# Normalising stage: units of four consecutive tokens, one bank and one copy for each half, loops written out

## What is computed

```python
h = h + _L0_attn_ref(_layernorm(h, axis=-1), gamma, W_in, b_in, conv_w, A, Bp, C, W_out, b_out)
h = h + _L0_ffn_ref(_layernorm(h, axis=-1), Ws, bs, W1, b1, W2, b2)

def _L0_attn_ref(x, gamma, W_in, b_in, ...):
    rms = jnp.linalg.norm(x, axis=-1, keepdims=True) * x.shape[-1] ** (-0.5)
    xn = gamma * (x / (rms + EPS))
    xp = xn @ W_in.T + b_in
    ...
```

## Time and profile before

| | us |
|---|---|
| median of three runs | 1370.59 |
| profiled execution: its time | 1371.16 |
| profiled execution: span of the trace | 1369.4 |
| TensorE busy in the span | 1150.6 (84%) |
| VectorE / ScalarE / GpSimd busy | 807.6 / 690.1 / 388.0 |
| normalising stage, from its first instruction to the next stage's first | 339.08 to 395.48 |

### The profile page before, as it was taken

How to read it: one execution, slowest core, us unless ns; L and a number is a source line. 1 busy time by engine, 2 the same in 40 slices (tenths; PEclk the granted TensorE clock), 3 DMA queues, 4 the chain that set the end, 5 groups by cost and what they waited for, 6 DMA issues and landing times. The chain is left out here.

```text
span 1369.4 us, 36841 instructions
## 1 busy us (share of the span) xinstructions
PE 1150.6 (84%) x11847; PEld 1087.9 (79%) x11847; DVE 807.6 (59%) x2553; ACT 690.1 (50%) x1544; POOL 388.0 (28%) x358
## 2 busy tenths in 40 slices
PE   0398994466579999999999499993899999999998
PEld 0298894344469899899997399993899999999998
DVE  0778977873842734535437268776455565666564
ACT  3165661255652333233233256563577777777775
POOL 6877000000100301202103024556133333323333
PEclk9999997685689999999999799996799999999999
DMA  8866412103510423234233789982111111111110
GB/s 189 187 95 145 116 37 60 34 0 118 220 27 2 107 67 98 63 98 102 63 95 71 223 251 298 286 268 86 31 47 44 43 44 42 46 43 46 43 46 21
DMA packets 166416, 133.70 MB, mean 98 GB/s; under 512 B 77989, under 2 KB 155932, under 8 KB 164704
## 3 DMA queue, kind: packets, MB, share of 16 engines
q1 hardware_dynamic: 152352, 112.22, 30.5%
q0 software_dynamic: 10384, 17.49, 4.1%
q10 hardware_dynamic: 3600, 3.01, 0.8%
HBM read 89.97 MB, written 43.53 MB: 97 GB/s over the span
## 5 line engine op out<-in xcount | busy, mean ns | idle before, releaser
L2132 POOL DMA_INDIRECT out_dram<-ob,oi x89 | 125.8, 1414 | 286.4 <-DVE ob L2186 281.0
L2242 PE MATMUL ph<-zt,wc 64*128 64x128 f32 x3204 | 198.5, 275 | 2.9 <-ACT zt L2144 1.4
L2242 PEld LDWEIGHTS ph<-zt,wc 64*128 64x128 f32 x3204 | 193.8, 191 | 4.9 <-ACT zt L2144 2.8
L2234 PE MATMUL py<-w2c,ht 64*128 64x192 f32 x2136 | 194.1, 327 | 1.6 <-DVE yb L2184 1.6
L1499 PE MATMUL pa<-wi,xn 96*85 96x96 f32 (+1 forms) x2048 | 186.6, 247 | 2.9 <-POOL mc L1351 2.9
L1499 PEld LDWEIGHTS pa<-wi,xn 96*85 96x85 f32 (+1 forms) x2048 | 181.6, 155 | 3.8 <-POOL mc L1351 3.1
L2157 ACT ACTIVATE ht<-ph,bc 128x128 f32<-128x128 f32 x534 | 156.9, 371 | 48.4 <-PE ph L2242 48.4
L2234 PEld LDWEIGHTS py<-w2c,ht 64*128 64x128 f32 x2136 | 172.6, 187 | 2.1 <-issue 1.3
L1362 POOL TENSOR_TENSOR bd<-rr,mc 128x656 f32<-128x656 f32 x48 | 61.6, 1282 | 291.0 <-PE pb L1517 171.2
L1373 DVE COPY x<-pa 85x384 f32<-85x384 f32 x100 | 55.3, 553 | 147.2 <-PE pa L1499 147.2
L341 PE MATMUL ps_y<-wg,xt 128*112 128x192 f32 x672 | 121.6, 332 | 14.2 <-DVE yg L431 13.8
(11 more groups left out here) (318 smaller groups left out, 1959.3 us busy)
## 6 DMA issues: line engine op xcount, KB each, us to landing
y<-yd SPq DMA_DIRECT2D x41, 384.0 KB, 4.1
gp<-kd SPq DMA_DIRECT2D x48, 246.0 KB, 2.8
xg<-in_x SPq DMA_DIRECT2D x16, 588.0 KB
xr<-xs SPq DMA_DIRECT2D x89, 98.0 KB, 1.9
yd<-yt SPq DMA_DIRECT2D x56, 144.0 KB, 1.9
hb<-h SPq DMA_DIRECT2D x41, 192.0 KB, 4.9
yd<-yt SPq DMA_DIRECT2D x40, 192.0 KB, 2.1
xg<-in_x SPq DMA_DIRECT2D x48, 112.0 KB
```

Source lines behind the costliest of these rows:

```text
L2132: pool.indirect_dma_start(out, bass.IndirectOffsetOnAxis(ap=oi[j][:, 0:1], axis=0), ob[j][:], None, bounds_check=bound, oob_is_err=False). ...
L2234: m = pe.matmul(py[h][:], ht[j][r, k, :], w2c[j % 2][r, k, :], start=(k == 0), stop=(k == FC - 1))
L2242: return pe.matmul(ph[c % 4][:, c // 4, :], wc[j][r, f:f + 128], zt[j][r, part, :], start=start, stop=stop, skip_group_check=True)
```

## The change

In `normalise_in` a unit becomes four consecutive tokens of a lane (lane 0: tokens 0 to 3 of a round of eight, lane 1: 4 to 7). There is one PSUM bank for each lane, parity of the round and half (`pz[j][m % 2][f]`, eight banks in place of four), and one copy takes a bank: four tokens of one half, 512 elements, written in runs of four neighbouring words of `xn` and read in PSUM with 128 words between the four. `z` has four tokens per buffer. The copies of a round run two rounds later (`take(m - 2)`, before one round later). The loops are written out, so that all addresses are constants, and `hold` goes. The statistics of the next part move on VectorE from the part's beginning to behind its second round. The moments and scales, the loads, GpSimd and the number of transposes stay.

```diff
-        z = [[sb(f"z4{j}{k}", [CB, 2, D]) for k in range(2)] for j in range(2)]
-        pz = [[bank(nc, ctx, f"pz{j}{k}", [HD, 4, CB]) for k in range(2)] for j in range(2)]
+        z = [[sb(f"z4{j}{k}", [CB, 4, D]) for k in range(2)] for j in range(2)]
+        pz = [[[bank(nc, ctx, f"pz{j}{k}{f}", [HD, 4, CB]) for f in range(2)] for k in range(2)] for j in range(2)]
...
+        def first_token(m, j):
+            return TS * m + 4 * j
+        def count(m, j):
+            return max(0, min(4, Q - first_token(m, j)))
+        def columns(m, j, f):
+            t = first_token(m, j)
+            return xn[0:HD, f, :, HALO:HALO + LP].rearrange("p b (c t) -> p b c t", c=NCHUNK)[:, :, :, t:t + count(m, j)]
+        def turned_tokens(m, j, f):
+            return pz[j][m % 2][f][:, 0:count(m, j), :].rearrange("p i (b c) -> p b c i", c=NCHUNK)
...
-            def take(m, k):
-                dve.wait_ge(turned[1], 2 * m + k + 1)
-                hold(dve, tick_d)
-                for i in range(2):
-                    c = dve.tensor_copy(scatter_cols(TS * m + 4 * k + 2 + i), turned_token(1, k, i))
-                c.then_inc(taken[1], 1)
+            def take(m):
+                for f in range(2):
+                    dve.wait_ge(turned[1], 2 * m + f + 1)
+                    dve.tensor_copy(columns(m, 1, f), turned_tokens(m, 1, f)).then_inc(taken[1], 1)
...
             statistics(0)
             scales(0)
-            make(0, 0)
-            make(0, 1)
             for n, (lo, hi) in enumerate(PARTS4):
                 if n:
                     scales(n)
-                more = n + 1 < len(PARTS4)
-                if more:
-                    statistics(n + 1)
-                if hi > 1:
-                    with dve.Fori(max(lo, 1), min(hi, NS4)) as m:
-                        for k in range(2):
-                            take(m - 1, k)
-                            make(m, k)
-            for k in range(2):
-                take(NS4 - 1, k)
+                for m in range(lo, min(hi, NS4)):
+                    if m >= 2:
+                        take(m - 2)
+                    make(m)
+                    if m == lo + 1 and n + 1 < len(PARTS4):
+                        statistics(n + 1)
+            for m in range(NS4 - 2, NS4):
+                take(m)
...
-                if not n:
-                    make(0, 0)
-                    make(0, 1)
-                if hi > 1:
-                    with act.Fori(max(lo, 1), min(hi, NS4)) as m:
-                        for k in range(2):
-                            take(m - 1, k)
-                            make(m, k)
-            take(NS4 - 1, 0)
-            make(NS4, 0)
-            take(NS4 - 1, 1)
-            take(NS4, 0)
+                for m in range(lo, hi):
+                    if m >= 2:
+                        take(m - 2)
+                    make(m)
+            for m in range(NS4 - 1, NS4 + 1):
+                take(m)
...
-            def turn(m, j, k):
-                pe.wait_ge(ready[j], 2 * m + k + 1)
-                pe.wait_ge(taken[j], 2 * m + k + 1)
-                for i in range(2):
-                    for f in range(2):
-                        t = pe.transpose(pz[j][k][:, 2 * i + f, :], z[j][k][:, i, f * HD:(f + 1) * HD], keep["ident"][:])
-                t.then_inc(turned[j], 1)
+            def turn(m, j):
+                pe.wait_ge(ready[j], m + 1)
+                for f in range(2):
+                    if m >= 2:
+                        pe.wait_ge(taken[j], 2 * (m - 2) + f + 1)
+                    for i in range(count(m, j)):
+                        t = pe.transpose(pz[j][m % 2][f][:, i, :], z[j][m % 2][:, i, f * HD:(f + 1) * HD], keep["ident"][:])
+                    t.then_inc(turned[j], 1)
```

More of the change, by code:

```diff
@@ L1070, in normalise_in @@
         ones = sem("ones4")
-        tick = keep["tick"]
-        tick_d = keep["tick_d"]
         block = ctx.enter_context(nc.Block(no_gpsimd_drain=True))
@@ L1140, in scales, with make @@
                 dve.wait_ge(zs_ok, n + 1)
-            def take(m, k):
-                dve.wait_ge(turned[1], 2 * m + k + 1)
-                hold(dve, tick_d)
-                for i in range(2):
-                    c = dve.tensor_copy(scatter_cols(TS * m + 4 * k + 2 + i), turned_token(1, k, i))
-                c.then_inc(taken[1], 1)
-            def make(m, k):
-                for i in range(2):
-                    t = TS * m + 4 * k + 2 + i
-                    c = ts(z[1][k][:, i, :], token(t), zs[:, bass.ds(t, 1)], nz[:, bass.ds(t, 1)], ALU.mult, ALU.add)
+            def take(m):
+                for f in range(2):
+                    dve.wait_ge(turned[1], 2 * m + f + 1)
+                    dve.tensor_copy(columns(m, 1, f), turned_tokens(m, 1, f)).then_inc(taken[1], 1)
+            def make(m):
+                for i in range(count(m, 1)):
+                    t = first_token(m, 1) + i
+                    c = ts(z[1][m % 2][:, i, :], h[:, t, 0:D], zs[:, t:t + 1], nz[:, t:t + 1], ALU.mult, ALU.add)
                 c.then_inc(ready[1], 1)
@@ L1179, in _, with take, make @@
         def _(act):
[L1180 to L1191, removed]
+            def take(m):
+                for f in range(2):
+                    act.wait_ge(turned[0], 2 * m + f + 1)
+                    act.activation(columns(m, 0, f), turned_tokens(m, 0, f), ACT.Copy).then_inc(taken[0], 1)
+            def make(m):
+                for i in range(count(m, 0)):
+                    t = first_token(m, 0) + i
+                    c = act.activation(z[0][m % 2][:, i, :], h[:, t, 0:D], ACT.Identity, scale=zs[:, t:t + 1],
+                                       bias=nz[:, t:t + 1])
                 c.then_inc(ready[0], 1)
@@ L1198, in _ @@
                 act.wait_ge(zs_ok, n + 1)
-                if not n:
-                    make(0, 0)
-                    make(0, 1)
-                if hi > 1:
-                    with act.Fori(max(lo, 1), min(hi, NS4)) as m:
-                        for k in range(2):
-                            take(m - 1, k)
-                            make(m, k)
-            take(NS4 - 1, 0)
-            make(NS4, 0)
-            take(NS4 - 1, 1)
-            take(NS4, 0)
+                for m in range(lo, hi):
[4 more added lines that the diff above has]
+                take(m)
         @block.tensor
         def _(pe):
-            def turn(m, j, k):
-                pe.wait_ge(ready[j], 2 * m + k + 1)
-                pe.wait_ge(taken[j], 2 * m + k + 1)
-                for i in range(2):
-                    for f in range(2):
-                        t = pe.transpose(pz[j][k][:, 2 * i + f, :], z[j][k][:, i, f * HD:(f + 1) * HD], keep["ident"][:])
-                t.then_inc(turned[j], 1)
[L1222 to L1228, removed]
+            def turn(m, j):
+                pe.wait_ge(ready[j], m + 1)
+                for f in range(2):
+                    if m >= 2:
[3 more added lines that the diff above has]
+                    t.then_inc(turned[j], 1)
+            for m in range(NS4):
+                for j in range(2):
+                    turn(m, j)
+            turn(NS4, 0)
 XU = CB // 4
```

## The result

The changed kernel took 1360.13 us (median of 12 runs, 1352.39 to 1363.22), the kernel before 1369.65 in the same series (12 runs, 1365.95 to 1374.49): the ratio is 0.9913, 95% interval 0.9898 to 0.9928. Measured once more on another occasion (the first kernel of the last experiment) the ratio was 0.9943, interval 0.9923 to 0.9964. The forecast was 1363.4, between 1360.5 and 1369.0: the direction was right, the first measurement lies 0.4 us under the range, the second one, 1362.91, inside. The forecast counts from 1370.59, the median of three runs; over the twelve the kernel before took 1369.65, so 0.9 of the 3.3 us between forecast and measurement lies in the start value. The gain itself was forecast at 7.2 us and measured at 9.5, and at 8.3 on the other occasion (1371.22 to 1362.91). The profiled execution of the change took 1361.33 us.

A forecast was written before the change was run, and what follows sets the result against it. ScalarE's sequence in the normalising stage was taken as the bound. Copies - 7.7, loops - 1.0, waits for scales + 1.0 and clock + 0.5 gave - 7.2 us: 1363.4 us from the median 1370.59, range 1360.5 to 1369.0.

The forecast's parts named there:

- The bound: Normalising stage after its head: ScalarE's sequence leads at 3.52 us a round, VectorE 0.44 us per round behind.
- Copies: PSUM copies into `xn`: 512 elements in 0.55 us on ScalarE, 0.68 on VectorE; 7.7 us less on ScalarE's path.
- The rival that they keep the price per element: Copies into `xn` stay at 0.92 and 0.99 us per 512 elements, gaining nothing: 1370 us, chance 0.12.
- The rival in which such a copy does not overlap with its follower: ScalarE's four-token copies hold the engine 1.38 us each: 9.7 us more, 1380 us, chance 0.05.
- Loops: Normalising stage: writing out the loops removes three entries on ScalarE, 1.0 us less.
- Waits for the scales: ScalarE's waits for `nz` at three changes of parts: 2.05, 2.55 and 1.9 against 1.84 us each, 1.0 us more.
- normalisations: Normalising stage: same counts and shapes, 0.42 us apart on ScalarE and 0.275 on VectorE, no change.
- the clock term: TensorE's transposes after changes of parts run at 1.2 GHz, and slow rounds cost 0.5 us more in all.
- the sum by terms: Normalising stage: - 7.7 - 1.0 + 1.0 + 0.5 = - 7.2 us, kept over the path's - 7.9.
- Following ScalarE instruction by instruction: Last part's times followed to the end: last copy at 386.8, or 387.3 with the clock's 0.5, against 395.16 us.
- its low end, 1361.4: Forecast case's own range, 1361 to 1366: with no alignment and no clock cost, 1361.4 us.
- the sentence that the next stage only starts earlier: Next stage starts as many microseconds earlier as ScalarE ends earlier; the change touches none of its own loads and table.

The follow-up runs named there:

- the first kernel of the last experiment: The changed kernel measured again with nothing altered, against the kernel before: ratio 0.9943 (0.9923 to 0.9964), 1362.91 us.
- The three kernels with extra transposes: Changed kernel plus unused TensorE transposes across the stage change, alone or with early scales and even-word runs, then also statistics first: ratios 0.9927, 0.9915, 0.9936 to before.
- the run with aligned runs: Changed kernel with one more padding column per sequence, so every run of four starts on an even word: 1356.03 us, run once.

## Why the prediction was wrong by a little

*The bound* was right: ScalarE's sequence, and it still is.

*Copies:* 0.55 and 0.68 us were forecast from the copy `y`, 0.535 and 0.605 measured. The rival that they keep the price per element (1370 us) is what the run with single words shows, 1369: the whole forecast hung on the order of the words, as it said. The rival in which such a copy does not overlap with its follower did not come: 1.07 us for two.

*Loops:* three entries fell from 0.39 to 0.03 us, 1.0 in all, as charged. The run with the loops alone gave 0.7.

*Waits for the scales:* forecast 2.05, 2.55 and 1.9 us. Measured from the end of ScalarE's normalisations to its first copy (the last normalisation starts the next instruction's turn 0.435 behind it): about 1.9, 2.8 and 1.9. The sum is right, in part by luck: VectorE's copies were cheaper than forecast, but VectorE waited for TensorE in the opening. In the repeat, where it did not, the second wait was 2.3.

*The first step that failed is the clock term,* 0.5 us for ScalarE's rounds behind a change of parts, with transposes at the low level. It rested on the earlier trace rows: after a pause of about 3 us the level is low. In the profile shown it was not:

```profile
366.89 1.95 PE L1206 MATMUL pz<-ident,z 128*96 128x128 f32 x16 [3.63 <-ACT z L1182]
```
```profile
366.00:368.00 2.00, 1.10 (x10) 1.00 0.03 8
```

After 3.63 us of pause sixteen transposes took 1.95 us at a granted clock of 1.00, the 2.4 GHz level. In the repeat of the same kernel, behind the same change of parts, it was:

```profile
363.85 1.18 ACT L1177 ACTIVATE xn<-pz 96x512 f32<-96x512 f32 x2
...
364.00 8.40 PE L1206 MATMUL pz<-ident,z 128*96 128x128 f32 x48 [3.17 <-ACT z L1182]
...
366.66 1.17 ACT L1177 ACTIVATE xn<-pz 96x512 f32<-96x512 f32 x2
```
```profile
366.00:368.00 2.00, 2.00 (x11) 0.50 0.00 0
```

Yet ScalarE's round there took 366.66 - 363.85 = 2.81 us, the same as at the high level, and in neither profile did a copy of ScalarE wait for TensorE. Two rounds of distance absorbed all of it: the term was nothing.

What a low level did cost came by a way that the prediction had not looked at, through VectorE in the opening. In the profile shown the clock was 0.50 up to 358:

```profile
356.00:358.00 2.00, 2.00 (x11) 0.50 1.05 453
```

VectorE's second pair of copies waited 0.35 us for its transposes, the statistics behind it came that much later, and ScalarE's third root waited 0.86 us for them. In the repeat, whose rounds begin 2.46 us earlier, the clock was 0.98 from 353 to 354 and 1.00 behind that, VectorE did not wait there, and the root waited 0.40:

```profile
359.22 0.24 ACT L1189 ACTIVATE vv<-vv 128x48 f32<-128x48 f32 x1 [0.40 <-DVE vv L1127]
```

That is nearly the whole difference between the two stages, 47.87 and 47.39 us.

*The second is the sum by terms itself.* Added up from start to start over ScalarE's timelines of the stage, before and in the profile shown, in us:

| part of ScalarE's path | forecast | measured |
|---|---|---|
| copies | -7.7 | -8.43 |
| normalisations | 0 | +0.47 |
| opening: wait for the first transposes | left out | -0.45 |
| loop entries and waits for the scales | -1.0 + 1.0 | -0.13 |
| clock, as ScalarE's wait for TensorE | +0.5 | 0 |
| sum | -7.2 | -8.5 |

The prediction says that ScalarE waits for nothing but `nz`. The trace before has one more wait, which goes because eight normalisations now come first:

```profile
352.72 1.17 ACT L1184 ACTIVATE xn<-pz 96x256 f32<-96x256 f32 x2 [0.39 <-PE pz L1219]
```

The normalisations, put at no change, stand 0.435 us apart in place of 0.42. Following ScalarE instruction by instruction gave 386.8 for its last copy's end without the clock's charge, 8.4 us less than before; measured it is 384.56 + 1.81 = 386.37, and 386.63 when counted from the same start (350.47 in place of 350.21). The path had the opening right and came close, but with copies 0.3 us too dear and normalisations 0.5 too cheap that nearly cancel. The forecast's own range mixes the two: its low end, 1361.4, comes out along the path, while by the terms it would be 1362.1.

*The third is the sentence that the next stage only starts earlier.* It also starts faster in the profile, by 1.2 us. Its clock was low from the first product on in the profile before (first line), and for less long after:

```profile
396.00:397.00 1.00, 0.31 (x2) 0.50 0.29 72
...
388.00:390.00 2.00, 2.00 (x18) 0.72 0.98 207
390.00:392.00 2.00, 2.00 (x15) 0.50 0.82 195
392.00:394.00 2.00, 2.00 (x24) 0.93 0.18 45
```

In the twelve profiles of this study that start took 11.06 to 11.52 us in the three whose copies write single words, 9.87 or 9.88 in three of the others and 8.24 to 8.45 in six; of the changed kernel itself once 9.88 and once 8.24. The three kernels with extra transposes all are among the six, but so are three without. So in every profile the kernels with runs of four start that stage at least 1.2 us faster than those with single words, and another 1.6 us comes and goes with the execution. What decides the level there stays open.

With 0.5 and 1.2 us corrected and the path in place of the sum, the forecast would have been - 8.4 - 1.2 = - 9.6 us, 1361.0 in terms of the median shown; the two measurements lie on either side of it.

## What to carry to other kernels

Before adding buffers or writing out loops around a copy, look at the order in which it writes: if neighbouring elements of a read land far apart, let a unit cover as many items as make a run of four words, and price the copy by another one in the trace that already writes such runs. Follow the leading engine instruction by instruction through the stage rather than adding up terms; the sum forgets the waits that the path shows. Do the same for the engine behind it where the leader waits for its results: here VectorE's 0.35 us of waiting reached ScalarE's path. And a stage that begins behind a meeting of all engines can start at either clock from one execution to the next, so a microsecond or two there belongs into the range.

## What the runs showed of the hardware that was not expected

- A copy's order alone: 512 elements from PSUM took 0.535 us on ScalarE and 0.605 on VectorE when written in runs of four words and read 128 words apart, and 0.96 and 0.98 when read in a row and written as single words 82 apart. No run changes the reading alone, but in the run with aligned runs a copy lasts 0.606 and 0.680 us on average, where a copy that reads and writes in a row lasts 0.593 and 0.686: the steps of the read do not show.
- Runs of four that start on an odd word in half of the cases cost ScalarE 0.04 us in 0.535, VectorE nothing.
- The same kernel in the same place kept TensorE's granted clock at 1.00 behind a pause of 3.63 us in one execution, and had it at 0.50 behind a pause of 3.17 in another; the kernel before had 0.50 behind 2.91.
